# Gathering the rest of expert 0 on TensorE in a gated cross-attention and mixture-of-experts kernel

## The reference

```python
x = x + tanh(g_xattn) * xattn(layernorm(x), ctx, ctx)       # gelu(x @ ctx.T) @ ctx, per batch
x = x + tanh(g_ffn)   * moe(layernorm(x), gate_w, gate_b, w1, b1, w2, b2)

def moe(x, gate_w, gate_b, w1, b1, w2, b2):                 # top 1 of 8 experts
    xf = x.reshape(-1, 256)
    top1 = argmax(xf @ gate_w.T + gate_b)
    for e in range(8):
        h = relu(xf @ w1[e].T + b1[e])                      # 256 -> 1024
        y = h @ w2[e].T + b2[e]                             # 1024 -> 256
        out = out + where(top1 == e, y, 0)
```

## Time and profile before

| | us |
|---|---|
| median of 3 runs | 110.49 (110.0 to 111.1) |
| profiled execution, its own time | 110.59 |
| span of that execution | 108.8 |
| TensorE matmuls busy | 98.6 (91%) |
| VectorE busy | 53.5 (49%) |
| ScalarE busy | 31.9 (29%) |
| GpSimd busy | 40.0 (37%) |

### The profile page before, as it was taken

The page is one execution under the profiler, slowest core; times in us unless marked ns, Lnnn a source line. Parts: engine busy times, 40 slices in busy tenths (PEclk is TensorE's granted clock), DMA queues, the critical chain, the costliest instruction groups (busy, mean ns, idle before and its releaser), DMA issues.

```text
span 108.8 us, 2102 instructions
## 1 busy us (share of the span) xinstructions
PE 98.6 (91%) x676; PEld 90.4 (83%) x677; DVE 53.5 (49%) x206; ACT 31.9 (29%) x98; POOL 40.0 (37%) x97
## 2 busy tenths in 40 slices
PE   5997999998996995999999999999999999999800
PEld 5986888887876893999999899899998998998600
DVE  0362787598588783898623324153223250433010
ACT  5616355554351440332304123023041230220000
POOL 3268687335376647702403473030030120300330
PEclk9999999999999999999999999999999999999998
DMA  3999999999995103699999999999991010010100
GB/s 76 328 378 395 423 431 419 410 422 405 394 420 199 54 0 98 172 382 358 397 405 401 428 405 370 418 424 428 425 409 68 6 44 0 0 40 6 48 23 31
DMA packets 6799, 28.66 MB, mean 264 GB/s; under 512 B 1150, under 2 KB 2560, under 8 KB 4737
## 3 DMA queue, kind: packets, MB, share of 16 engines
q1 hardware_dynamic: 4752, 25.40, 58.2%
q0 software_dynamic: 864, 2.12, 6.4%
q10 hardware_dynamic: 1168, 0.98, 2.8%
HBM read 26.64 MB, written 2.11 MB: 264 GB/s over the span
## 4 chain that ended last, share of the span: by engine, by line
PE 66%; DVE 12%; DMA 7%; POOL 5%; issue 4%; SPq 1%; ACT 1%; POOLq 0%; DVEq 0%
PE bank L996 26%; PE bank L1005 26%; PE bank L946 6%; PE bank L935 4%; DMA x<-in_x 4%; DMA region<-x_rows,from_row 3%; DVE x L593 2%; PE bank L978 2%; DVE stats L609 2%; DVE cand L642 1%; DVE lg L632 1%; PE bank L925 1%; POOL mv L290 1%; POOL out_rows L388 1%; DVE first L647 1%
## 5 line engine op out<-in xcount | busy, mean ns | idle before, releaser
L996 PE MATMUL bank<-region,w 128*128 128x128 f32 x288 | 34.8, 277 | 0.9 <-ACT region L493 0.9
L996 PEld LDWEIGHTS bank<-region,w 128*128 128x128 f32 x288 | 33.8, 192 | 1.4 <-ACT region L493 0.9
L1005 PE MATMUL bank<-w,region 128*128 128x256 f32 x144 | 32.6, 380 | 0.0
L1005 PEld LDWEIGHTS bank<-w,region 128*128 128x128 f32 x144 | 26.7, 191 | 3.2
L529 ACT ACTIVATE region<-bank,smalls 128x128 f32<-128x128 f32 x40 | 12.5, 363 | 40.0 <-PE bank L996 40.0
L388 POOL DMA_INDIRECT out_rows<-region,to_row x9 | 8.9, 988 | 34.6 <-DVE region L838 33.2
L822 DVE TENSOR_SCALAR region<-bank,smalls 128x128 f32<-128x128 f32 x32 | 9.6, 346 | 13.6 <-PE bank L996 13.0
L383 POOL DMA_INDIRECT region<-x_rows,from_row x9 | 9.4, 1046 | 15.3 <-DMA region<-x_rows,from_row 12.0
L838 DVE SCALAR_TENSOR_TENSOR region<-bank,tg,region 128x256 f32<-128x256 f32 (+1 forms) x9 | 4.4, 484 | 20.9 <-PE bank L1005 20.9
L935 PEld LDWEIGHTS bank<-w,region 128*128 128x128 f32 x96 | 11.8, 192 | 1.0 <-DVE w L584 0.2
L946 PE MATMUL bank<-region,w 128*112 128x272 f32 x48 | 12.4, 394 | 0.0
(11 more groups left out here) (119 smaller groups left out, 81.7 us busy)
## 6 DMA issues: line engine op xcount, KB each, us to landing
w<-in_w1t SPq DMA_DIRECT2D x8, 1024.0 KB, 21.0
w<-in_w2t SPq DMA_DIRECT2D x8, 1024.0 KB, 23.0
region<-in_ctx SPq DMA_DIRECT2D x5, 792.0 KB, 11.7
region<-in_ctx SPq DMA_DIRECT2D x3, 408.0 KB, 7.2
region<-in_ctx SPq DMA_DIRECT2D x3, 384.0 KB, 4.4
x_rows<-x ACTq DMA_DIRECT2D x8, 113.8 KB, 6.5
b2b<-in_b SPq DMA_DIRECT2D x1, 896.0 KB, 12.0
x<-in_x_rest SPq DMA_DIRECT2D x1, 670.0 KB, 6.1
```

The lines of the kernel that those rows point to most:

```text
L996: mm = pe.matmul(hT_ps[k][:, part % 2 * P:(part % 2 + 1) * P], w1[:, e, n * H + part * P:n * H + (part + 1) * P], xgT[:, j % 2, n * P:(n + ...
L1005: mm = pe.matmul(y[:, 0:D], hidT[:, q, part, :], w2[:, e, part * D:(part + 1) * D], start=(part == 0), stop=(part == KH - 1))
```

## The change

Block 1, the tokens of expert 0 from batches 3 to 7, is now gathered on TensorE as well, by one-hot products over five batches (`gather_first`); for this VectorE normalises all eight batches itself (`norm_x2`), and GpSimd (batches 3 to 5) and VectorE (6, 7) make the one-hot columns. Its row gather by DMA stays, for the residual, and moves to third place: the order is 2, 0, 1, 3, 4, ... Block 0 has 64 columns instead of 128 (`gather_small`, `up_small`); its down product has w2 as stationary and the 64 hidden columns as moving operand, in 16 products, and two transposes turn the result back (`down_small`, `turn_small`). Tokens of class 0 numbered 64 and up are moved to rank 128 and up, so into overflow (`move_far`, `cnt_add`; MAX_OVER becomes 7). Batches 4, 5 and 6, 7 are routed in pairs. Batches 0 to 2 are routed after batch 2 instead of 3, and their rank products stand after the attention product of batch 4 instead of after the scores of batch 6. GpSimd does the inverse deviation of batch 2 before its constants. up(0) and down(0) are complete before the row numbers are made; up(1), down(1), up(2) follow, with the turn of block 3 three quarters into up(2). SP waits for the products that gather block 1 and for the row gather of block 2, and loads expert 7 after the first finished block.

```diff
-MAX_OVER = CHUNKS - 1
+MAX_OVER = CHUNKS
+SMALL_BLOCK = 64
@@ sync
             sp.wait_ge(xnT_done, B)
-            sp.wait_ge(xgT_done, 1)
-            sp.wait_ge(first_in[1], 16)
+            sp.wait_ge(xgT_done, 2)
             sp.wait_ge(xg_in[0], 16)
             load_expert(2)
...
-            for e in range(3, E):
+            for e in range(3, E - 1):
                 load_expert(e)
+            sp.wait_ge(y_done, 1)
+            load_expert(E - 1)
@@ gpsimd
+            def pick_expert_0(b):
+                pool.wait_ge(rank_ok, 2)
+                pool.wait_ge(is_e0_ok, 3)
+                pool.tensor_scalar(pick_x[0:S, b - EARLY, :], iota_r[0:S, :], rank[0:S, b:b + 1], is_e0[0:S, b:b + 1],
+                                   ALU.is_equal, ALU.mult).then_inc(pick_mid_ok, 1)
...
+            of_x(2)
+            std_of_x(2)
             pool.memset(ones[:], 1.0).then_inc(pool_step, 1)
...
             of_x2(4)
+            pick(0, 1)
+            pick(1, 1)
             running_count(4)
-            pick(0, 1)
+            pick(2, 1)
             of_x2(5)
-            pick(1, 1)
-            pick(2, 1)
             running_count(5)
             running_count(6)
+            place()
             of_x2(6)
             of_x2(7)
-            pick(3, 2)
-            pick(4, 2)
-            running_count(7)
-            place()
-            pick(5, 3)
+            for b in range(EARLY, 6):
+                pick_expert_0(b)
+            for b in range(EARLY, 6):
+                pick(b, 2)
...
-            for j in (1, 2, 0, *range(3, BLOCKS)):
+            for j in (2, 0, 1, *range(3, BLOCKS)):
@@ scalar
-                if b == B - 1:
-                    first_halves()
+            small_copy()
+            small_relu(0)
+            small_relu(1)
             store_x2(B - 1)
+            small_relu(2)
+            small_relu(3)
+            yT_copy()
+            first_halves()
...
-            relu(0, 0, 0, later=False, pairs=range(4))
-            xgT_copy(1, 1)
-            relu(1, 1, 0, later=False)
+            relu(1, 1, 0, later=False, pairs=range(4))
             xgT_copy(2, 0)
@@ vector
             for b in range(B):
                 if b == 6:
-                    route(5, 1, 4)
+                    route(4, 2, 3)
                 add_attention(b)
                 stats_x2(b)
                 join_x2(b)
-                if 1 <= b <= EARLY:
+                if 1 <= b <= 5:
                     norm_x2(b - 1)
...
-                if b == 3:
-                    dve.wait_ge(consts_ok, 12)
+                if b == 2:
+                    dve.wait_ge(consts_ok, 13)
                     route(0, 3, 1)
-                    is_expert_0()
                 if b == 4:
+                    own_count(0, 3, 1)
+                    rank_of(0, 3, 1, rank0_ok)
+                    move_far()
                     route(3, 1, 2)
-                    own_count(0, 3, 1)
-                    rank_of(0, 3, 1)
-                if b == 5:
-                    route(4, 1, 3)
-                if b == 6:
-                    own_count(3, 2, 2)
-                    rank_of(3, 2, 2)
-            add_last_logits()
...
+            norm_x2(5)
+            own_count(3, 3, 2)
+            rank_of(3, 3, 2, rank_ok)
+            norm_x2(6)
+            route(6, 2, 4)
+            norm_x2(7)
+            own_count(6, 2, 3)
+            rank_of(6, 2, 3, rank_ok)
+            for b in (6, 7):
+                pick_expert_0(b)
+            for b in (6, 7):
+                pick(b)
+            place(6, 2)
@@ tensor
+            def gather_small():
+                for k in range(KD):
+                    for b in range(EARLY):
+                        pe.wait_ge(pick_s_ok, b + 1)
+                        pe.wait_ge(xn2_ok, b + 1)
+                        mm = pe.matmul(xs_ps[:, k * SMALL_BLOCK:(k + 1) * SMALL_BLOCK], xn2[0:S, b, k * P:(k + 1) * P],
+                                       pick_s[0:S, b, :], start=(b == 0), stop=(b == EARLY - 1))
+                mm.then_inc(xgT_done, 1)
+            def gather_first(b):
+                pe.wait_ge(xn2_ok, b + 1)
+                for k in range(KD):
+                    mm = pe.matmul(x1_ps[k][:, 0:P], xn2[0:S, b, k * P:(k + 1) * P], pick_x[0:S, b - EARLY, :],
+                                   start=(b == EARLY), stop=(b == B - 1))
...
+            def up_small():
...
+                    for n in range(KD):
+                        mm = pe.matmul(hTs_ps[part // 2][:, part % 2 * SMALL_BLOCK:(part % 2 + 1) * SMALL_BLOCK],
+                                       w1[:, 0, n * H + part * P:n * H + (part + 1) * P],
+                                       xgT[:, 0, n * SMALL_BLOCK:(n + 1) * SMALL_BLOCK], start=(n == 0), stop=(n == KD - 1))
...
+            def down_small(k):
+                for part in range(KH):
...
+                    mm = pe.matmul(yT_ps[:, k * SMALL_BLOCK:(k + 1) * SMALL_BLOCK],
+                                   w2[:, 0, part * D + k * P:part * D + (k + 1) * P], hidT[:, 0, part, 0:SMALL_BLOCK],
+                                   start=(part == 0), stop=(part == KH - 1))
...
                 if b + 1 < B:
                     scores(b + 1)
-                if b == 5:
-                    pe.wait_ge(consts_ok, 12)
-                    rank_sums(0, 3)
                 if b + 2 < B:
                     turn_xn(b + 2)
                 attend(b)
-                if b == 6:
-                    pe.wait_ge(oh_ok, 3)
-                    rank_sums(3, 2)
+                if b == 4:
+                    pe.wait_ge(consts_ok, 13)
+                    pe.wait_ge(oh_ok, 1)
+                    rank_sums(0, 3)
+            gather_small()
+            pe.wait_ge(oh_ok, 3)
+            rank_sums(3, 3)
+            up_small()
+            pe.wait_ge(pick_mid_ok, 1)
+            pe.wait_ge(x2_ok, B)
+            gather_first(3)
+            pe.wait_ge(rank_read, 2)
+            pe.wait_ge(w2_in[0], 16)
+            down_small(0)
...
+            down_small(1)
+            pe.wait_ge(pick_mid_ok, 2)
+            gather_first(4)
...
+            gather_first(7)
...
+            up(1)
+            turn_small()
+            down(1, 1, 0, range(0, KH - 2))
             turn_block(2, 0)
+            down(1, 1, 0, range(KH - 2, KH))
             up(2, range(0, KH // 2))
...
             mm.then_inc(tok_done, 1)
+            up(2, range(KH // 2, KH - 2))
+            turn_block(3, 1)
+            up(2, range(KH - 2, KH))
-            for j in range(1, E - 1):
-                if j >= 2:
-                    up(j + 1)
+            for j in range(2, E - 1):
+                up(j + 1)
                 turn_block(j + 2, j % 2)
```

More of the change, by code:

```diff
@@ L354, in _ @@
             pool.memset(cum[:, 0, :], 0.0).then_inc(consts_ok, 1)
-            for b in range(2, 6):
+            pool.memset(cnt_add[:], 0.0).then_inc(pool_step, 1)
+            pool.wait_ge(pool_step, 8)
+            pool.memset(cnt_add[:, 0:1], float(P - SMALL_BLOCK)).then_inc(consts_ok, 1)
+            for b in range(3, 6):
                 of_x(b)
@@ L666, in route @@
                 one_hot(b, n, group)
+                is_expert_0(b, n, group)
             def own_count(b, n, group):
@@ new lines, in pick_expert_0, with place @@
+            def pick_expert_0(b):
+                dve.wait_ge(rank_ok, 3)
+                dve.wait_ge(is_e0_ok, 4)
+                dve.tensor_scalar(pick_x[0:S, b - EARLY, :], iota_r[0:S, :], rank[0:S, b:b + 1], is_e0[0:S, b:b + 1],
+                                  ALU.is_equal, ALU.mult).then_inc(pick_end_ok, 1)
+            def place(b, n):
+                dve.wait_ge(oh_ok, 4)
+                dve.tensor_tensor(pick_e0[0:S, b:b + n, :], oh[0:S, b:b + n, :],
+                                  idw[0:S, b:b + n].unsqueeze(2).to_broadcast([S, n, C]),
+                                  ALU.mult).then_inc(place_last_ok, 1)
@@ new lines, in down_small @@
+            def down_small(k):
+                for part in range(KH):
+                    if k == 0:
+                        pe.wait_ge((hTa_ok, hTd_ok)[part // 2 % 2], part // 4 * 2 + part % 2 + 1)
+                    mm = pe.matmul(yT_ps[:, k * SMALL_BLOCK:(k + 1) * SMALL_BLOCK],
+                                   w2[:, 0, part * D + k * P:part * D + (k + 1) * P], hidT[:, 0, part, 0:SMALL_BLOCK],
+                                   start=(part == 0), stop=(part == KH - 1))
+                if k == KD - 1:
+                    mm.then_inc(yT_done, 1)
@@ L971, in tokens, with turn_small @@
+            def turn_small():
+                pe.wait_ge(yT_ok, 1)
+                for k in range(KD):
+                    mm = pe.transpose(ys_ps[0:SMALL_BLOCK, k * P:(k + 1) * P],
+                                      yT[:, k * SMALL_BLOCK:(k + 1) * SMALL_BLOCK], ident[:])
+                mm.then_inc(y_done, 1)
             def tokens(b):
-                return pe.matmul(tok0_ps[:, 0:C], pick_r0[0:S, b, :], pick_e0[0:S, b, :],
```

(20 more changed lines are left out.)

213 lines of the change are left out of this document (109 added, 104 removed).

## The result

The kernel after took 125.4 us (median; 124.47 to 126.92) against 110.64 us for the kernel before in the same comparison: a ratio of 1.131, 95% interval 1.121 to 1.141. I had forecast slower, 113.7 us, and a range up to 115.1. The direction was right; more than three quarters of the loss (11.6 of 14.8 us) were not in the sum.

What follows compares the result with a forecast made beforehand. TensorE, busy 91% of the span, was taken as the bound; up(4) moving from 63.4 to 66.6 us gave +3.2 on 110.59, 113.8, less 0.1 to the median: 113.7 us; likeliest range 112.4 to 114.7, with rivals 110.0 to 115.1.

Steps and rivals of the forecast that it cites:

- Price of a record with 64 columns: Small block's products on TensorE: the weight load sets each record at 0.110 us, despite half the columns.
- rival B: Columns set the 64-column record, 0.057 us, in the up and down products of block 0; 110.2 us, chance 0.12.
- Start: GpSimd does batch 2's deviation before its constants, so TensorE's wait before batch 2's turn goes: -0.58 us.
- Rank products of batches 0 to 2: Moved ahead of batch 6's scores, they make TensorE wait 2.1 us for the running counts; batch 5's attention +0.95 us.
- To the up product of block 0: VectorE's chain from batch 5's attention product to block 0's up product; start at 35.45 us instead of 34.43.
- To the row numbers: TensorE's work from block 0's up product to the row numbers: 10.2 us, so they come at 45.6 instead of 38.15.
- Behind F: F is when row numbers are read; 1.75 us of new wait at block 3's turn, up(4) at F+21.0, 66.6 us.
- rival D: The fourth row gather lands later still, since weight loads start ahead of it; up to 1.3 us, 115.1 us, chance 0.06.
- The limit by w1 of expert 3: Second limit on up(4): this weight load lands at F+20.9, 66.5 us, its earlier lead of 3.5 us used up.
- A: Rival: fast fourth gather and weights 2 us sooner lift both limits behind F; up(4) F+19.1, 111.8 us, chance 0.1.
- C: Rival: running counts come without a wait in the attention loop, everything to F 2.1 us earlier; 111.6 us, chance 0.08.
- The floor: TensorE gains 2.2 us of work against 3.0 us of waits, so the gain is at most 0.8 us.

Runs made afterwards that it cites:

- e2_fill: The kernel after plus six products on a zero tile in TensorE's 1.35 us wait ahead of up_small; 117.8 us, ratio 1.066.
- e12_best_pad: e10_best with the small block's 64 columns streamed twice, as 128; 111.47 us, ratio 1.007.
- e9_rank: The kernel after with the rank products of batches 0 to 2 moved back behind the scores of batch 6; 124.37 us, ratio 1.128.
- e7_early: e2_fill with block 3's rows gathered second and normalised earlier, and experts 2 and 3 loaded right after the small gather; 113.22 us, ratio 1.025.
- e8_all: e7_early with the rank products of batches 0 to 2 back behind the scores of batch 6; 111.87 us, ratio 1.012.
- e13_copy: The kernel after with ScalarE copying the small gathered block ahead of the store of batch 6; 116.84 us, ratio 1.046.
- e1_pad: The kernel after with the 64 columns streamed twice, as 128, in up_small and down_small; 118.35 us, ratio 1.066.
- e10_best: e8_all with e13_copy's earlier copy instead of the filling products, and the overflow's table products one quarter of up(2) later; 111.52 us, ratio 1.009.
- e11_before64_fill: The kernel before with 64 columns in block 0's up products and four zero products in the 0.86 us wait ahead; 111.02 us, ratio 1.002.
- e3_order: The kernel after with row gathers in the order 2, 3, 0, 1, 4, so block 3's is second; 126.95 us, ratio 1.146.

## Why the prediction was wrong, point by point

- **Price of a record with 64 columns**: right. 0.113 us at full clock where I took 0.110; rival B (0.057) is out, by e2_fill and by e12_best_pad.
- **Start**: right, the turn of batch 2 came at 10.21 without a wait.
- **Rank products of batches 0 to 2**: right in place, 0.7 us too dear. I had 2.1 us of wait, it was 1.42: the pause of 0.51 us in the counts didn't recur, and batch 3's addition was at 22.15. Moving them back gave 1.1 us (e9_rank), between e7_early and e8_all 1.35.
- **To the up product of block 0**: right, 35.02 for 35.45.
- **To the row numbers**: this step failed. I summed 10.2 us, all at the full clock, because the trace of before had the full clock everywhere; measured were 17.7 (35.02 to 52.71). In e2_fill and e13_copy the same list took 10.21 us each (35.81 to 46.02, 34.75 to 44.96), so the list and its prices were right and the clock was the whole difference, 7.5 us. I looked at the wait ahead of `up_small` as time lost, and at the narrow products as bound by their weights, and put the effect of the two on the clock at nothing, without a reason. What the runs show: with wide products behind it a wait of 0.85 us let the clock be (before), and one of 1.34 us took it down for 3.4 us (e1_pad, in the longest of its executions); with narrow products behind the 1.35 us it went down and stayed down until 53.7 us, five microseconds into products of 128 columns (from 48.67). With the wait shortened to 0.30 us it didn't fall in this stretch of the profiled execution.
- **Behind F**: I had up(4) at F+21.0; it was F+24.6 (52.71 to 77.33). The stall at the turn of block 3 was where I had put it, but 3.35 us instead of 1.75: block 3 was normalised at F+14.1 instead of F+12.2. That is rival D, which I had priced at up to 1.3 us and which came to 2.0: the fourth gather was issued at 58.12, one microsecond behind the first weight load (57.08); before, it was issued at 43.54, ahead of the first (43.79). That the loads hold it back is argued from this order; no run moves them alone. The other 1.6 us are again the clock: behind this stall it fell a second time, and 40 records of full products took 5.87 us (67.79 to 73.66) instead of 4.46. The limit by w1 of expert 3 wasn't reached, since the stall had pushed up(4) past it, but it too was priced too low: w1 was issued at 58.4 and landed 16.3 us later, at 74.7, which is F+22.0 instead of F+20.9.
- The sum over these: +3.2 forecast, -0.4 up to `up_small`, +7.5 to the row numbers, +3.6 behind them, 13.9 as measured.
- **Rivals**: A is out (the fourth gather is late in every run that leaves it fourth, F+13.6 to F+14.3). C did not happen. None of them had the clock in it. Two of their sums were off as well: A's own list adds up to F+19.25 instead of F+19.1, and A with B to some 108.4 us instead of 108.1. The Trainium skill's page "TensorE: Matmul & The Clock Gate", section "What's actually happening", says that the low clock is the default and activity releases it, and puts its two levels down to an idle and a busy engine. The rows agree on the two levels (1.00 and 0.50) and differ on busy: the profile has TensorE without a gap for 17 us at the lower one. With twice the columns in the same records (e1_pad) the clock was back 13 us sooner.
- The floor I had given (2.2 us more work than before, where 3.0 us of waits could go) was reached by no run. In e10_best, at full clock, TensorE is busy for 100.1 us, 1.5 more than before. It took 111.5 us, still 0.9% above the kernel before, and its padded twin e12_best_pad 0.7%; none beat it.

Not settled: whether narrow products bring the clock down without any idle time ahead of them. In e2_fill they follow wide ones without a gap, and the clock stays full for 11 us; in e11_before64_fill the wait of 0.86 us is filled and the clock still falls in five of ten executions, with one wait of 0.23 us left in the stretch. So a shorter fall takes less than a wait of 1.35 us ahead of narrow products, and how much less the runs don't show.

## What to carry to other kernels

In this kernel a record with 64 moving columns on 128 columns of float32 weights took as long as one with 128 (0.113 and 0.112 us). Halving the columns gained nothing, and behind a wait of 1.35 us the clock was at half for 17 us of such a stretch, in which the profile shows the engine busy. When such products are added, look at the row of the granted clock first, and see to it that no wait stands ahead of them: here one copy, moved ahead of a store on ScalarE, was worth 8.6 us. And before a sum made at one clock is trusted, ask for every wait of the order of a microsecond what work follows it.

## What the runs showed that I had not expected

- The clock went to half behind a wait of only 1.35 us, and stayed there through 17 us in which TensorE was busy without a gap.
- In or right behind a stall of 3.3 to 4.0 us at the turn of block 3 it fell even though wide products followed, and came back after 2.9 us of them in the kernel after, 4.4 us in e1_pad (63.1 to 67.5) and 5.2 us in e13_copy (59.5 to 64.7). One execution of e13_copy had a mean clock of 0.996 and took 114.78 us, so this fall isn't certain each time.
- A gather of 128 rows landed 2.8 to 3.5 us behind its issue when it was the first or second (before, e2_fill, e3_order). As the fourth it took 6.7 us in the kernel before, issued just ahead of the first weight load, and 8.8 to 8.9 us in e2_fill and e3_order, issued behind it.
